# A four-layer graph network on one core: prologue, hand-overs and last store put in another order

## The chip, the core and the metric

The kernel runs on one core of a Trainium2 chip. The core has TensorE (matrix products, with a separate weight load that overlaps them), VectorE, ScalarE, GpSimd, and SyncE, whose queue here issues every DMA. Results of TensorE land in eight banks of 128 x 512 fp32. The metric is the device time of one execution in microseconds, as the median of several.

## The reference, cut to what matters

x is 128 graphs of 64 nodes with 512 features, fp32; adj is 128 matrices of 64 x 64. Four layers follow, each `x = x + layer(relu(layernorm(x)), adj)`:

```python
# layer 0:  w = ISQ * sum_d q * (adj @ k)          q, k = h @ Wqk;  x += softmax_nodes(w) * (h @ Wv)
# layer 1:  p = adj * exp(query @ key.T)           query, key, value with biases;  x += (p / rowsum(p)) @ value
# layer 2:  8 heads of 64: softmax(q @ k.T / 8 * (adj + adj)) @ v, with biases, then Wo and bo
# layer 3:  e = leaky_relu(sj + si + ab);  P = adj * exp(e) / rowsum;  H = h@Wk0 + P@h@Wk1 + P@P@h@Wk2 + sum(bk)
#           x += relu(H);   si, sj = (h @ Wv + bv) @ aw
```

The kernel folds weights: layer 0 needs only m0 = Wq Wk^T, layer 1 only a1 = Wk^T Wq with the vectors crow (from bq and Wk) and ucol (from bk and Wq) and the number s0 = bq . bk. In layer 3, sj and si come from two sums of h against two rows ("sums").

## The kernel before, in words

The 8192 rows are worked through in 16 groups of 512 (NG = 16), a group as 4 tiles of 128 rows, that is 8 graphs. Layers 0 and 1 go through one loop (group g of layer 0 beside group g - 1 of layer 1), then a loop of layer 2, then one of layer 3; x goes to memory in between (mid). Every engine has a program of its own, written out by hand in order, and waits on counting semaphores. Banks are taken strictly in turn, eight in rotation: whoever takes a bank waits until the use eight takes earlier was read out (`Banks.take`, line 51).

An fp32 product of full accuracy is made from three fp32r passes: each operand is split into a high part (ScalarE's copy, line 973) and a low part, the rest (VectorE, line 615, or GpSimd, lines 1204 and 1222); `gemm_T` (line 317) and `gemm` (line 327) run hi*hi, hi*lo, lo*hi. The prologue instead uses plain fp32 products, which are two records each in the trace (line 307).

The features go from x through statistics (VectorE, 627 and 629), a scale (GpSimd, 1209 to 1214), a normalising copy (ScalarE, 987), VectorE's transposes of 32 x 32 blocks (648), a gather by 16 DMAs (1406), then the high and low split, to the products.

The places that the change touches:

- Prologue of TensorE (lines 386 to 411): 32 transposes of Wqk in two halves (294), all copied out by ScalarE into qT and kTw; the small biases; product m0; s0; two row vectors (409) of bcol against wk1 and wq1; two of the four parts of a1. Round 0 then runs G0 (the first products of layer 0) and v0; at its end come the other two parts of a1, the transposes of Wv1, and the two row vectors are spread into crow (470) and ucol (474).
- Prologue of GpSimd: the low split of Wv0 (1240) before that of h0T (1241).
- Last round of layers 0 and 1 (g == NG): Wq2 is transposed and split, then `l01_pv` of group 14, then the last g1 (layer 1's product against a1), then Wk2 is transposed and split, then the last v1.
- Layer 2's scores (484): two calls, each for two tiles, each over all four feature blocks of q and k.
- Layer 2's last round: VectorE makes the sums of tiles 2 and 3 of group 0 (961), then adds the bias into the values VV (893), against which TensorE runs ctx (528).
- Layer 3: the sums go out to memory (`sums_out3`, 1431) and come back spread over all partitions (`sums_in3`, 1438); VectorE adds them (zct, 832), ScalarE takes exp, GpSimd multiplies with adj (alt), TensorE takes row sums (582), VectorE divides (900, 902), GpSimd scales (ttt, 1324), then Thi (ScalarE) and Tlo (VectorE), which the first hop (588) needs. The sums of group 1 are made in two pieces, one before layer 3's first low split Z_lo, one behind the row sums. On SyncE's queue the sums go out behind the next group's x load (`load3`) and four block loads.
- The last store is one DMA of 1 MB behind the last of four tiles.

Of the kernel before, what the change touches and what calls it, by code (L numbers as in the profile page):

```python
# [74 lines left out]
def build(nc, x, adj, nodemask, L0_gnn_Wqk, L0_gnn_Wv, L1_gnn_Wq_w, L1_gnn_Wq_b, L1_gnn_Wk_w, L1_gnn_Wk_b,  # L75
# [14 lines left out]
    with root:  # L90
# [20 lines left out]
        d_o = sems("x_out0 x_out1 x_out2 x_out3")  # L111
        d_adj = sems("adj_in0 adj_in1")
# [8 lines left out]
        (c_pool, a_whi, v_wlo, p_wlo, a_qkT) = sems("consts_pool w_hi w_lo_dve w_lo_pool qkT")  # L121
        (v_mcol, v_rows1, v_crow, v_ucol, p_one1) = sems("mcol rows1 crow ucol ones_v")
# [65 lines left out]
        urow, crow1 = alloc(tmp, "urow", [1, 512]), alloc(tmp, "crow1", [1, 512])  # L188
# [73 lines left out]
        def x_slot(k):  # L262
            return k % 4
# [22 lines left out]
        def pe_program(eng):  # L286
# [99 lines left out]
            pe.wait_ge(c_pool, 1)  # L386
            for half in range(2):
                pe.wait_ge((d_qk0, d_qk1)[half], 16)
                for cc in range(4):
                    transposed_blocks(("qkT", half, cc), wqk[:, :, half * 512:(half + 1) * 512], cc, (a_qkT, 4 * half + cc + 1))  # L390
# [6 lines left out]
            pe.wait_ge(a_qkT, 8)  # L397
            product("m0", qT, kTw)
            b, full, before = bank.take(("s0",), (v_rows1, 1))
# [27 lines left out]
            for g in range(NG + 1):  # L427
# [3 lines left out]
                else:  # L431
# [5 lines left out]
                    split_T("q2", Wq2["raw"])  # L437
                if on_pv:
                    l01_pv(g - 2)
# [10 lines left out]
                if on1:  # L450
# [12 lines left out]
                else:  # L463
                    product("a1", wk1, wq1, (2, 3))
                    pe.wait_ge(d_v1, 16)
                    split_T("v1", wv1)
                    b, full, before = bank.take(("crow",), (v_crow, 1))
                    pe.wait_ge(*before)
                    pe.wait_ge(v_rows1, 3)
                    eng.matmul(b[:], ones1[0:1, :], crow1[:], start=True, stop=True).then_inc(full, 1)  # L470
# [1132 lines left out]
```

## Time and profile before

| | |
|---|---|
| three runs | 2316.1, 2312.76, 2315.93 us; median 2315.93 |
| the profiled execution | 2312.03 us, of which 2310.2 are the span |
| TensorE busy | 2287.1 us, 99% of the span |
| VectorE, ScalarE, GpSimd busy | 57%, 32%, 30% |
| mean granted TensorE clock | 0.998 of full speed |
| DMA | 209.01 MB, mean 90 GB/s |
| chain that ended last | TensorE 93%, VectorE 2%, SyncE's queue 2%, rest 3% |

All times in the trace are microseconds from the span's start; 1.83 us of the execution lie around the span. A record's length overlaps with its neighbour's on TensorE, so there the distance between starts is what one costs.

### The profile page before, as it was taken

The numbers are of one execution on the slowest core, as the hardware profiler recorded it, in microseconds if no ns is written. First come the engines' busy times: TensorE is split into PE (matmuls) and PEld (weight loads), VectorE is DVE, ScalarE is ACT, GpSimd is POOL, SyncE is SP. The second block draws the span as 40 slices with busy tenths as digits, with TensorE's granted clock in tenths as the row PEclk, the third lists the DMA queues.
The fourth block names the chain that finished last, engine by engine and source line by source line (L and its number), as shares of the span: only waits on it lengthen the run. The fifth ranks groups of instructions, "written<-read, shape, count | busy, mean of one in ns | idle before, by whom it ended". The sixth has DMA issues, their size and how long they took to land.

```text
span 2310.2 us, 39569 instructions
## 1 busy us (share of the span) xinstructions
PE 2287.1 (99%) x16015; PEld 1860.6 (81%) x16015; DVE 1318.4 (57%) x2745; ACT 747.8 (32%) x1333; POOL 700.2 (30%) x930
## 2 busy tenths in 40 slices
PE   8999999999999999999999999999999999999998
PEld 5788788888878877888888888888778888888887
DVE  3565565656556555545554445555686757676753
ACT  3332323333233333333333333333433232323221
POOL 2433333343333322233322223332342121212120
PEclk9999999999999999999999999999999999999999
DMA  6323333333333343222232222222353333333330
GB/s 198 77 76 95 109 101 83 93 91 87 95 108 105 97 124 105 61 60 67 80 93 60 60 61 60 72 85 95 95 142 94 98 94 97 95 97 96 96 78 37
DMA packets 173479, 209.01 MB, mean 90 GB/s; under 512 B 64800, under 2 KB 81264, under 8 KB 173296
## 3 DMA queue, kind: packets, MB, share of 16 engines
q1 hardware_dynamic: 173296, 206.48, 32.0%
q8 instruction: 126, 2.06, 0.4%
q14 instruction: 57, 0.47, 0.1%
HBM read 88.91 MB, written 50.37 MB: 60 GB/s over the span
## 4 chain that ended last, share of the span: by engine, by line
PE 93%; DVE 2%; SPq 2%; ACT 1%; issue 1%; DMA 1%; POOL 0%; DVEq 0%; ACTq 0%
PE bank L327 50%; PE bank L317 29%; PE bank L588 4%; PE bank L343 3%; SPq L1406 2%; PE bank L528 1%; PE bank L501 1%; PE bank L307 1%; PE bank L378 1%; PE bank L511 1%; PE bank L294 0%; DVE hs L648 0%; DVE yt L961 0%; ACT g1T L1022 0%; PE bank L409 0%
## 5 line engine op out<-in xcount | busy, mean ns | idle before, releaser
L327 PE MATMUL bank<-w_hi,h3T_hi 128*128 128x512 f32 x768 | 302.4, 394 | 0.0
L327 PE MATMUL bank<-w_hi,h3T_lo 128*128 128x512 f32 x768 | 299.5, 390 | 0.0
L327 PE MATMUL bank<-w_lo,h3T_hi 128*128 128x512 f32 x768 | 299.5, 390 | 0.0
L615 DVE TENSOR_TENSOR Z_lo<-bank,Z_hi 128x512 fp32r<-128x512 f32 x128 | 87.1, 682 | 181.6 <-ACT Z_hi L973 181.3
L987 ACT ACTIVATE hn<-x,stA 128x512 f32<-128x512 f32 x192 | 140.7, 804 | 99.3 <-POOL stA L1214 99.3
L327 PEld LDWEIGHTS bank<-w_hi,h3T_hi 128*128 128x128 f32 x768 | 144.6, 188 | 30.2
L327 PEld LDWEIGHTS bank<-w_lo,h3T_hi 128*128 128x128 f32 x768 | 144.4, 188 | 30.2
L327 PEld LDWEIGHTS bank<-w_hi,h3T_lo 128*128 128x128 f32 x768 | 144.4, 188 | 30.2
L973 ACT ACTIVATE Z_hi<-bank 128x512 fp32r<-128x512 f32 x128 | 76.1, 596 | 251.1 <-PE bank L327 159.6
L1209 POOL TENSOR_SCALAR stA<-stA 128x4 f32<-128x4 f32 x48 | 11.5, 241 | 448.1 <-DVE stA L629 446.9
L615 DVE TENSOR_TENSOR cT_lo<-bank,cT_hi 128x256 fp32r<-128x256 f32 x128 | 44.7, 409 | 179.7 <-ACT cT_hi L973 179.7
L1222 POOL TENSOR_TENSOR h3T_lo<-hGA,h3T_hi 128x512 fp32r<-128x512 f32 x64 | 80.8, 1295 | 202.6 <-ACT h3T_hi L973 202.6
L1222 POOL TENSOR_TENSOR h1T_lo<-hGB,h1T_hi 128x512 fp32r<-128x512 f32 x64 | 80.7, 1293 | 201.2 <-ACT h1T_hi L973 201.2
L627 DVE BATCH_NORM_STATS2 stA<-x 128x6 f32<-128x512 f32 x192 | 128.2, 668 | 9.7 <-DMA x<-mid 9.1
L648 DVE STREAM_TRANSPOSE hs<-hn 128x512 f32<-128x512 f32 x192 | 120.6, 682 | 10.2 <-ACT hn L987 9.8
L805 DVE TENSOR_TENSOR x<-bank,x 128x512 f32<-128x512 f32 x64 | 43.3, 677 | 135.2 <-PE bank L327 132.1
L973 ACT ACTIVATE g0T<-bank 128x512 f32<-128x512 f32 x64 | 38.3, 598 | 239.9 <-PE bank L317 239.9
L327 PE MATMUL bank<-v_hi,h0T_hi 128*128 128x512 f32 x256 | 104.5, 408 | 0.0
L327 PE MATMUL bank<-o2w_hi,cT_hi 128*128 128x512 f32 x256 | 103.5, 404 | 0.5 <-DVE cT_lo L615 0.5
L1286 POOL TENSOR_TENSOR x<-x,blk 128x512 f32<-128x512 f32 x64 | 80.7, 1299 | 73.3 <-ACT hn L987 73.3
L317 PE MATMUL bank<-h1T_hi,a_hi 128*128 128x512 f32 x256 | 99.8, 390 | 2.4 <-POOL h1T_lo L1222 2.4
L317 PE MATMUL bank<-h0T_hi,m_hi 128*128 128x512 f32 x256 | 101.7, 397 | 0.0
(222 smaller groups left out, 5824.9 us busy)
## 6 DMA issues: line engine op xcount, KB each, us to landing
hGA<-hs SPq DMA_DIRECT2D x768, 64.0 KB, 2.0
mid<-x SPq DMA_DIRECT2D x32, 1024.0 KB, 4.8
x<-mid SPq DMA_DIRECT2D x32, 1024.0 KB, 5.8
x<-in_x SPq DMA_DIRECT2D x16, 1024.0 KB, 5.7
hGB<-hs SPq DMA_DIRECT2D x256, 64.0 KB, 2.0
out<-x SPq DMA_DIRECT2D x16, 1024.0 KB, 5.4
blk<-in_adj SPq DMA_DIRECT2D x128, 64.0 KB
adj<-in_adj SPq DMA_DIRECT2D x64, 64.0 KB, 3.3
```

Source lines behind the costliest of these rows:

```text
L317: ins = eng.matmul(b[:], W[l][:, k, os], h[r][:, k, :], start=(k == 0 and i == 0), stop=(k == 3 and i == 2))
L327: ins = eng.matmul(b[:], h[l][:, k, ts], W[r][:, k, :], start=(k == 0 and i == 0), stop=(last and k == 3 and i == 2))
L343: ins = eng.matmul(b[h, t * 64:(t + 1) * 64], left[:, k, ts], right[:, 2 * i:2 * i + 2, 4 * k + t, :], start=(k == 0), stop=(k == 3))
L588: ins = eng.matmul(b[:], T[g % 2][l][:, t, :], Z[zi][r][:, t, :], start=False, stop=(i == 2))
L615: return eng.tensor_tensor(lo, src, hi.bitcast(F), ALU.subtract)
L627: m = dve.step(eng.bn_stats(st[:, t, 0:6], xt[:, t, :]))
L648: eng.transpose(hs[:, :, :, t, :].rearrange("p b c r -> p c b r"), (hn1 if layer == 1 else hn)[t][:].rearrange("p (c b r) -> p c b r", c=4 ...
L973: return eng.activation(dst, src, ACT.Copy)
L987: eng.activation(h[t][:], xt[:, t, :], ACT.Relu, bias=st[:, t, 10:11], scale=st[:, t, 9:10]).then_inc(done, 1)
L1222: eng.tensor_tensor(by_token(h["lo"], q), hG[:, q], by_token(h["hi"], q).bitcast(F), ALU.subtract).then_inc(done, 1)
L1286: eng.tensor_tensor(xt[:, t, :], xt[:, t, :], bo2, ALU.add).then_inc(p_xb, 1)
L1406: eng.dma_start(hG[b * 32:b * 32 + 32, q].rearrange("p c r -> p (c r)"), hs[q * 32:q * 32 + 32, b].rearrange("p c t r -> p (c t r)")).then ...
```

## The change

What it does, part by part:

1. TensorE transposes the unit matrix 20 times into a bank that nobody reads, before it waits for Wqk. The k half of Wqk is copied out by VectorE, the q half by ScalarE as before.
2. crow comes at once in all partitions, from 4 products with a broadcast column as weights; ucol comes as columns, from 16 products with one column each. The two row vectors and what was done with them at the end of round 0 fall away.
3. One part of a1 instead of two is made before G0, three instead of two behind it. GpSimd splits h0T before Wv0.
4. Wk2 is transposed and split right behind Wq2, ahead of `l01_pv` and g1, on TensorE, VectorE and ScalarE.
5. Scores: one call for all four tiles, which runs the first two feature blocks for all tiles, then the last two, and waits for q and k by halves.
6. In layer 2's last round the values are added before the sums; the sums of layer 3's group 1 are made in one piece.
7. Sums go out ahead of the loads on SyncE's queue. The last group's store is four DMAs of 256 KB, one behind each tile.

Lines in parentheses stand for several.

```diff
@@ pe_program
             pe.wait_ge(c_pool, 1)
+            b, full, _ = bank.take(("idle",), (c_pool, 1))
+            for i in range(20):
+                ins = eng.transpose(b[:, 0:128], ident[:], ident[:])
+            ins.then_inc(full, 1)
             for half in range(2):
                 pe.wait_ge((d_qk0, d_qk1)[half], 16)
                 for cc in range(4):
-                    transposed_blocks(("qkT", half, cc), ..., cc, (a_qkT, 4 * half + cc + 1))
+                    transposed_blocks(("qkT", half, cc), ..., cc, ((a_qkT, v_qkT)[half], cc + 1))
...
-            pe.wait_ge(a_qkT, 8)
+            pe.wait_ge(a_qkT, 4)
+            pe.wait_ge(v_qkT, 4)
             product("m0", qT, kTw)
...
-            for j, (w, loaded, c0) in enumerate(((wk1, d_k1, 0), (wq1, d_q1, 4))):
-                b, full, before = bank.take(("rows1", j), (v_rows1, 2 + j))
-                pe.wait_ge(*before)
-                pe.wait_ge(loaded, 16)
+            b, full, before = bank.take(("crow",), (v_crow, 1))
+            pe.wait_ge(*before)
+            pe.wait_ge(d_k1, 16)
+            for k in range(4):
+                ins = eng.matmul(b[:], bcol[:, k:k + 1].to_broadcast([128, 128]), wk1[:, k, :], start=(k == 0), stop=(k == 3))
+            ins.then_inc(full, 1)
+            b, full, before = bank.take(("ucol",), (v_ucol, 1))
+            pe.wait_ge(*before)
+            pe.wait_ge(d_q1, 16)
+            for d in range(4):
                 for k in range(4):
-                    ins = eng.matmul(b[0:1, :], bcol[:, c0 + k:c0 + k + 1], w[:, k, :], start=(k == 0), stop=(k == 3))
-                ins.then_inc(full, 1)
-            product("a1", wk1, wq1, (0, 1))
+                    ins = eng.matmul(b[:, d:d + 1], wq1[:, k, d * 128:(d + 1) * 128], bcol[:, 4 + k:5 + k], start=(k == 0), stop=(k == 3))
+            ins.then_inc(full, 1)
+            product("a1", wk1, wq1, (0,))
...
                     split_T("q2", Wq2["raw"])
+                    pe.wait_ge(d_k2, 16)
+                    split_T("k2", Wk2["raw"])
                 if on_pv:
                     l01_pv(g - 2)
...
-                    if g == NG:
-                        pe.wait_ge(d_k2, 16)
-                        split_T("k2", Wk2["raw"])
                     l01_v1(g - 1, 0)
...
-                    product("a1", wk1, wq1, (2, 3))
+                    product("a1", wk1, wq1, (1, 2, 3))
                     pe.wait_ge(d_v1, 16)
                     split_T("v1", wv1)
-                    (crow: ones1[0:1, :] x crow1; ucol: four urow x ones1[0:1, 0:1])
...
-            def l2_scores(g, u):
+            def l2_scores(g):
                 bs = []
-                for r in range(2):
+                for r in range(4):
...
-                pe.wait_ge(a_q, 4 * g + 4)
-                pe.wait_ge(a_k, 4 * g + 4)
-                for x_ in range(2):
-                    t = 2 * u + x_
-                    for mm in range(2):
+                for mm in range(2):
+                    pe.wait_ge(a_q, 4 * g + 2 * mm + 2)
+                    pe.wait_ge(a_k, 4 * g + 2 * mm + 2)
+                    for t in range(4):
                         for a in range(2):
...
                             for s in range(2):
                                 for p in range(2):
-                                    h, m, (b, full) = HALF[p], 2 * mm + s, bs[p]
+                                    h, m, (b, full) = HALF[p], 2 * mm + s, bs[2 * (t // 2) + p]
...
-                                    if x_ == 1 and mm == 1 and a == 1 and s == 1:
+                                    if mm == 1 and t % 2 == 1 and a == 1 and s == 1:
                                         ins.then_inc(full, 1)
@@ dve_program
+            for cc in range(4):
+                dve.wait_ge(*bank.done(("qkT", 1, cc)))
+                eng.tensor_copy(kTw[:, cc, :], bank.of(("qkT", 1, cc))[:]).then_inc(v_qkT, 1)
             dve.wait_ge(*bank.done(("cols",)))
...
-            for j, row in enumerate((crow1, urow)):
-                dve.wait_ge(*bank.done(("rows1", j)))
-                eng.tensor_copy(row[:], bank.of(("rows1", j))[0:1, :]).then_inc(v_rows1, 1)
-            split_W(Wa1, "a1", (0, 1))
+            (crow and ucol copied here instead of at the end of round 0)
+            split_W(Wa1, "a1", (0,))
...
                     split_W(Wq2, "q2")
+                    split_W(Wk2, "k2")
                 if on_pv:
                     l01_x2(g - 2)
...
                 if on1:
                     adj_T(0, g - 1)
-                    if g == NG:
-                        split_W(Wk2, "k2")
...
                 if not on:
-                    l3_sums(dve, eng, 1, (0, 1))
+                    l3_sums(dve, eng, 1, range(4))
                 if on:
                     dve.wait_ge(d_bv2, 16)
-                    if g == NG - 1:
-                        l3_sums(dve, eng, 0, (2, 3))
                     for t in range(4):
                         (the additions of bv2 into VV)
+                    if g == NG - 1:
+                        l3_sums(dve, eng, 0, (2, 3))
...
                     if g == 0 and t == 0:
                         l3_rowsum(0)
-                        l3_sums(dve, eng, 1, (2, 3))
@@ act_program
-            for half, dst in enumerate((qT, kTw)):
-                for cc in range(4):
+            for cc in range(4):      (qT alone)
...
                     features2_hi(1, NG - 1, hT[1], (3,))
+                    split_W(Wk2, "k2")
...
                         g1(g - 1)
-                    if g == NG:
-                        split_W(Wk2, "k2")
@@ pool_program
+            features_lo(0, 0, hT[0], hGA, p_flo0)
             split_in_place(Wv0, "v0")
-            features_lo(0, 0, hT[0], hGA, p_flo0)
@@ sp_program
                         sp.wait_ge(*bank.done(("wT", "a1", 3)))
-                        sp.wait_ge(*bank.done(("rows1", 1)))
+                        sp.wait_ge(*bank.done(("ucol",)))
...
             for g in range(NG):
+                sums_out3(g + 1)
                 load3(g + 2)
                 load_blocks(3, g + 1)
-                sums_out3(g + 1)
                 sums_in3(g + 1)
                 gather(3, g + 2)
-                sp.wait_ge(v_x4, 4 * g + 4)
-                store_x(kA(3, g), out_v[g])
+                if g + 1 < NG:
+                    sp.wait_ge(v_x4, 4 * g + 4)
+                    store_x(kA(3, g), out_v[g])
+            for t in range(4):
+                sp.wait_ge(v_x4, 4 * (NG - 1) + t + 1)
+                eng.dma_start(out_v[NG - 1][:, t, :], xs[x_slot(kA(3, NG - 1))][:, t, :]).then_inc(d_last, 16)

```

## Rows read from the trace of the kernel before

**Rows 1.** TensorE's waits: releaser, then total us, times, longest us.

```profile
PE bank L317 <- POOL h1T_lo L1222: 2.4, 2, 1.6
PE bank L528 <- DVE VV L893: 2.3, 1, 2.3
PE bank L588 <- DVE Tlo L615: 2.3, 1, 2.3
...
PE bank L317 <- DVE h2T_lo L615: 0.7, 1, 0.7
```

**Rows 2.** Timeline of TensorE, 0 to 140 us: start, length, line, operation.

```profile
5.83 5.67 PE L294 MATMUL bank<-ident,wqk 128*128 128x128 f32 x32 [5.83 <-DMA wqk<-in_L_gnn_Wqk]
...
12.34 14.00 PE L307 MATMUL bank<-kTw,qTw 128*128 128x512 f32 x32 [0.49 <-ACT kTw L973]
...
26.38 3.59 PE L409 MATMUL bank<-wk,bcol 128*1 128x512 f32 x8
...
33.34 7.13 PE L307 MATMUL bank<-wq,wk 128*128 128x512 f32 x16
39.91 0.79 PE L317 MATMUL bank<-h0T_hi,m_hi 128*128 128x512 f32 x1
...
73.62 1.12 PE L470 MATMUL bank<-crow,ones 1*128 1x512 f32 x2
74.58 0.94 PE L474 MATMUL bank<-ones,urow 1*128 1x1 f32 x8
75.45 0.50 PE L317 MATMUL bank<-h0T_hi,m_hi 128*128 128x512 f32 x1
```

**Rows 3.** Timeline of ScalarE, 5.7 to 12.4 us, one row of four.

```profile
8.66 0.60 ACT L973 ACTIVATE qTw<-bank 128x512 f32<-128x512 f32 x1 [0.25 <-PE bank L294]
```

**Rows 4.** Windows: busy time by engine, granted clock, DMA share, GB/s.

```profile
6.70:7.60 0.90, 0.90 (x6) 0.90 (x6) 0.00 (x0) 0.60 (x1) 0.00 (x0) 1.00 1.04 385
```

**Rows 5.** Source view of the two loads of Wqk, time from issue.

```profile
L1443 SPq DMA_DIRECT2D wqk<-in_L_gnn_Wqk x2: 445/470/496, 0.7 to 1.2; - x2
...
DMA to landing us min/median/max: 5.0/6.1/7.2
```

**Rows 6.** Timeline of all engines, 0 to 75 us, GpSimd.

```profile
32.48 4.95 POOL L1222 TENSOR_TENSOR h0T_lo<-hGA,h0T_hi 128x512 fp32r<-128x512 f32 x4
```

**Rows 7.** Timelines of ScalarE and VectorE, 828 to 925 us.

```profile
839.74 0.63 ACT L973 ACTIVATE h1T_hi<-hGB 128x512 fp32r<-128x512 f32 x1 [0.20 <-DMA hGB<-hs]
...
854.77 2.48 DVE L615 TENSOR_TENSOR k2w_lo<-bank,k2w_hi 128x512 fp32r<-128x512 f32 x4 [4.58 <-PE bank L294]
```

**Rows 8.** Timelines, 1600 to 1740 us, and a window of line 961 alone.

```profile
1682.42 0.87 DVE L832 TENSOR_TENSOR zct<-sirows,stB 64x256 f32<-64x256 f32 x2 [1.15 <-DMA sirows<-si]
...
1684.80:1687.40 2.60, 2.54 (x8) 1.00 0.46 107
...
1692.09 0.85 ACT L973 ACTIVATE Thi<-ttt 64x256 fp32r<-64x256 f32 x2 [3.22 <-POOL ttt L1324]
...
1697.71 1.41 DVE L615 TENSOR_TENSOR Tlo<-ttt,Thi 64x256 fp32r<-64x256 f32 x2
```

**Rows 9.** SyncE's queue: two issues near 1670 us, its waits after 1800 us.

```profile
1663.30 0.37 SPq L1431 DMA_DIRECT2D si<-stB  x1
...
1676.19 0.62 SPq L1438 DMA_DIRECT2D sirows<-si  x1
...
SPq L1438 <- DMA si<-stB: 122.9, 12, 12.8
```

**Rows 10.** Timelines of TensorE and VectorE, 886 to 915 and 990 to 1064 us.

```profile
894.58 2.09 PE L501 MATMUL bank<-KK,QQ 64*64 64x64 f32 x128 [0.87 <-ACT KK L1101]
...
1006.53 3.00 DVE L615 TENSOR_TENSOR h2T_lo<-hGA,h2T_hi 128x512 fp32r<-128x512 f32 x4
...
1012.34 0.48 PE L317 MATMUL bank<-h2T_hi,q2w_hi 128*128 128x512 f32 x1
```

**Rows 11.** Source view of the last three stores.

```profile
DMA to landing us min/median/max: 4.3/4.3/5.0
```

More of the change, by code:

```diff
@@ L111, in build @@
         d_o = sems("x_out0 x_out1 x_out2 x_out3")
+        (d_last,) = sems("last_out")
         d_adj = sems("adj_in0 adj_in1")
@@ L396, in pe_program @@
             eng.transpose(b[:, 64:72], brow1[:], ident[0:8, 0:8]).then_inc(full, 1)
-            pe.wait_ge(a_qkT, 8)
+            pe.wait_ge(a_qkT, 4)
+            pe.wait_ge(v_qkT, 4)
             product("m0", qT, kTw)
-            b, full, before = bank.take(("s0",), (v_rows1, 1))
+            b, full, before = bank.take(("s0",), (v_s0, 1))
             pe.wait_ge(*before)
@@ L463, in pe_program @@
                 else:
-                    product("a1", wk1, wq1, (2, 3))
+                    product("a1", wk1, wq1, (1, 2, 3))
                     pe.wait_ge(d_v1, 16)
                     split_T("v1", wv1)
[L467 to L470, printed above, removed]
-                    b, full, before = bank.take(("ucol",), (v_ucol, 1))
-                    pe.wait_ge(*before)
-                    for d in range(4):
-                        ins = eng.matmul(b[:, d:d + 1], urow[:, d * 128:(d + 1) * 128], ones1[0:1, 0:1], start=True, stop=True)
-                    ins.then_inc(full, 1)
             def l2_gemm_T(n, g, W, freed):
@@ L563, in pe_program @@
                 if on:
-                    for u in range(2):
-                        l2_scores(g, u)
+                    l2_scores(g)
                 if prev:
@@ L722, in dve_program @@
             dve.wait_ge(*bank.done(("s0",)))
-            eng.tensor_reduce(s0, bank.of(("s0",))[:, 0:4], AX, ALU.add).then_inc(v_rows1, 1)
-            for j, row in enumerate((crow1, urow)):
-                dve.wait_ge(*bank.done(("rows1", j)))
-                eng.tensor_copy(row[:], bank.of(("rows1", j))[0:1, :]).then_inc(v_rows1, 1)
-            split_W(Wa1, "a1", (0, 1))
+            eng.tensor_reduce(s0, bank.of(("s0",))[:, 0:4], AX, ALU.add).then_inc(v_s0, 1)
+            dve.wait_ge(*bank.done(("crow",)))
+            eng.tensor_copy(crow[:], bank.of(("crow",))[:]).then_inc(v_crow, 1)
+            dve.wait_ge(*bank.done(("ucol",)))
+            eng.tensor_copy(ucol, bank.of(("ucol",))[:, 0:4]).then_inc(v_ucol, 1)
+            split_W(Wa1, "a1", (0,))
             for g in range(NG + 1):
@@ L785, in dve_program @@
                 else:
-                    dve.wait_ge(*bank.done(("crow",)))
-                    eng.tensor_copy(crow[:], bank.of(("crow",))[:]).then_inc(v_crow, 1)
-                    dve.wait_ge(*bank.done(("ucol",)))
-                    eng.tensor_copy(ucol, bank.of(("ucol",))[:, 0:4]).then_inc(v_ucol, 1)
                     l01_dots(0)
@@ L1030, in norm_B @@
                     norm(hn1, stB, p_stB, 4 * g + t + 1, a_nB, xs[x_slot(kA(0, g))], t)
-            for half, dst in enumerate((qT, kTw)):
-                for cc in range(4):
-                    act.wait_ge(*bank.done(("qkT", half, cc)))
-                    copy(dst[:, cc, :], bank.of(("qkT", half, cc))[:]).then_inc(a_qkT, 1)
+            for cc in range(4):
+                act.wait_ge(*bank.done(("qkT", 0, cc)))
+                copy(qT[:, cc, :], bank.of(("qkT", 0, cc))[:]).then_inc(a_qkT, 1)
             norm_A(0, 0)
```

24 lines of the change are left out of this document (12 added, 12 removed).

## The prediction

> **What bounds the kernel now.** I read the page's busy shares first (in the table above: TensorE 99%), then the list of what TensorE waited for, then TensorE's own order of instructions in the prologue, and last the other engines' timelines around each wait. The reader is to see two things. TensorE is the bound nearly everywhere, so an edit pays only where it takes away a TensorE instruction, takes away one of its few waits, or shortens what lies before its first or behind its last instruction. And the waits are few and single: four rows of the list carry most of what can be won inside the kernel [rows 1], the longest single ones being 1.6, 2.3, 2.3 and 0.7 us. The prologue is 39.9 us of TensorE work before the first big product [rows 2].
>
> **The prologue, step by step.** *Unit transposes and the split copies.* The 32 transposes of Wqk start at 5.83, when its first half has landed, and product m0 starts at 12.34 [rows 2]. ScalarE copied one bank of four transposes in 0.60 us and then waited 0.25 us for TensorE [rows 3], so the first transposes came at 0.85/4 = 0.21 us each. All 32 took 5.67 us, so the second 16 took about 2.3 us, 0.14 each. The same instruction became quicker while TensorE was kept busy, so I take it that 20 unit transposes, run while the load is under way, let all 32 go at the quick pace. The granted clock of that early stretch is shown as 1.00, the 2.4 GHz level [rows 4]; by that row alone nothing was held back, unit transposes would change nothing, and only the second engine for the copies would be left, some 0.2 us. The Trainium skill (TensorE: Matmul & The Clock Gate, "What's actually happening") says that the array's clock starts at the lower level, 1.2 GHz, and is released by sustained activity; by that rule the step is worth the whole 0.6 that follows. The quick pace puts the q half at 8.1. The k half was issued about 0.5 us after the first (0.72) and the longest landing is 7.2 us [rows 5]: it is there at about 8.4, so its 16 transposes end at 10.6. Its copies are now VectorE's; a 128x512 tile out of a bank goes there at 2.48/4 = 0.62 us [rows 7], so four from 9.1 end at 11.6, and m0 starts at 11.7: **0.6 us gained** (bounds 0 and 1.5, the whole difference in pace).
>
> *Biases by columns.* Now two rows of 4 products (16 records) take 33.34 - 26.38 = 6.96 us, 0.435 each [rows 2]. After: the broadcast crow is 8 such records, 3.5 us; ucol is 16 products of one column, 32 records. The nearest row is the old ucol, also 128 weight columns against one column: 8 records from 74.58 to 75.45, 0.109 each [rows 2], so 32 cost 3.5 us. Sum 7.0: **nothing gained**. Bounds: the weights had one row there and have 128 now, so twice the price is possible (3.5 lost); free, it would be 3.5 gained. What was done with the results at the end of the first round, 73.62 to 75.45 [rows 2], goes: **1.83 us gained**.
>
> *One part of a1 ahead of G0.* Two parts take 39.91 - 33.34 = 6.57 us [rows 2]. One of them moves from before G0 to behind it: nothing gained or lost, if G0 can start 0.6 + 3.3 us earlier, at 36.0. GpSimd's low part of h0T ends at 32.48 + 4.95 = 37.4 now [rows 6], 1.4 us too late, but it stood behind four equally long pieces of Wv0 and is put ahead of them; it can then be held by ScalarE and the gather alone, about 1.2 us (one of its four pieces) behind the last slice. Wv0's pieces end 5 us after that, under G0's 48 matmuls (at half of a1's 0.41 us a record still 9.8 us). The cover of the first is thin: without it 1.4 us are lost.
>
> **Wk behind Wq.** The last g1 waits 1.6 us for h1T_lo [rows 1]; 16 transposes at 0.109, 1.75 us, are moved into that hole. But their banks come free only through ScalarE's high and VectorE's low parts, and g1's first bank now is that of k2's third. ScalarE ends its last h1T slice at 840.37 [rows 7]; then 0.6 for k2's first high part and three low parts of 0.62 make 842.9 with the semaphores. Now g1 can start behind one low piece of 1.24 us on GpSimd [rows 6], at 841.7. So 1.75 - 1.2 = **0.5 us gained** (0 to 1.75). VectorE's x2 behind it comes 3 us later; its stores have a round to go.
>
> **Scores.** Only round 0 waits for KK, 0.87 us of the 2.09 us row [rows 10]. The first half of the scores can now run in that wait. VectorE gets its first two banks after 3/4 instead of 1/2 of the scores, about 895.1 instead of 895.6, and the next thing late is h2T_lo at the end of VectorE's softmax (0.7 us wait [rows 1]), which moves by that 0.5: **0.45 us gained** (0 to 0.87). In the other 15 rounds the same order costs VectorE 0.5 us; h2T_lo ends at 1006.53 + 3.00 = 1009.5 and TensorE asks for it at 1012.34 [rows 10], 2.8 us later, so nothing.
>
> **Values ahead of sums, sums together, sums sent first.** The 2.3 us wait for VV goes, as VectorE adds the four values (4 x 0.62) first. But TensorE then reaches the wait for Tlo (2.3 us [rows 1]) sooner, and what ends that wait is not TensorE's. Its chain: the sums go out at 1663.30, come back by a load issued at 1676.19 [rows 9], zct runs at 1682.42 as soon as they land; later Thi is ready at 1692.94, but Tlo starts only at 1697.71 and ends at 1699.12 [rows 8], since four sums stand between. So 4.8 us of the chain are sums. Moved ahead of the row sums, four cost 2.5 us where GpSimd is quiet [rows 8]; part of that falls into time in which VectorE waits there for TensorE, and I take 2.0 (bounds 0 and 2.5) by which Thi comes later; Tlo follows at once: 4.8 - 2.0 = **2.8 us gained**, not 2.3 + 2.3. Values first sends the sums 2.5 us later, about 1666; the return load stood 12.9 us behind them on SP, while a later round's return waited 122.9/12 = 10.2 us on average, 12.8 at most [rows 9], so it can still leave near 1676. Bounds: 0.4 (12.8 us out, so return 2.4 later) and 5.6 (return 2.8 earlier, with TensorE no longer held). In later rounds SP now stands for the sums before its next x load and four block loads, about 1.5 us; TensorE needs neither for most of a round.
>
> **Store by tiles.** The last store, 1 MB, lands 4.3 us after its issue [rows 11]; the last quarter, 256 KB, lies between a quarter of that, 1.1, and the whole. Some of a transfer surely does not shrink with its size, so I take 2.5, a little under the middle: **1.8 us gained** (0 to 3.2). Only the last of the four is in the way; the others leave while TensorE still works. The Trainium skill speaks against the split (DMA: Bandwidth & Descriptors, "Bandwidth"): batch transfers to 1 MiB or more, small ones waste most of their time. By that rule the four would cost more together, and the term were 0 if that reached the last; by the page's fit of 2.0 us and bytes over 436 GB/s, an estimate, the last falls from 4.4 to 2.6 us, again 1.8.
>
> **Sum:** 0.6 + 0 + 1.83 + 0.5 + 0.45 + 2.8 + 1.8 = 8.0 us. On the profiled execution's own 2312.0 that gives 2304.0. The median of the three runs, 2315.9, lies 3.9 above that execution; on it the sum gives 2307.9. The forecast lies between, **2306**.
>
> **Rivals.** *The hand-over is released wholly:* the sums return 3 us earlier, TensorE alone sets the first hop, 5.6 instead of 2.8: gain 11, about 2303. For it: SP reaches the return load sooner once the x stores move up. Against it: two 1 MB transfers share that stretch. *The sums' way through memory eats the hand-over:* out 2.5 us later and 12.8 us under way, return 2.4 later, 0.4 instead of 2.8: gain 5.6, 3.8 if the tail gives nothing: 2308.5 to 2310. *ucol's weight loads cost double:* gain 4.5, 2309.5; for it, a full 128 rows were never loaded against one column in a long row here. *Slower:* the new score order breaks the overlap of the small products. 128 records take 2.09 us, 16 ns each, against 0.109 us for lone small products; at 32 ns each a round costs 2.1 us more, 34 us in 16 rounds: 2340. It decides from 0.8 us a round on (8.0 + 4.6 over 16). Against it: the four innermost products that run beside each other stay as they were.
>
> **Chances and range.** Forecast case 0.58; released wholly 0.10; sums eat it 0.20; ucol double 0.07; slower 0.05. A measurement can tell 0.2%, 4.6 us, from no change. Faster: 0.58 + 0.10 + 0.12 of the third case = 0.80; same: 0.08 + 0.07 = 0.15; slower 0.05. Low end: the second case on the profiled execution, 2301; high end: the small gains on the median, 2311.5.
>
> **What would show it.** Right: ScalarE's and VectorE's Wqk copies side by side, m0 at 11.7, G0 near 36, round 1's G0 near 73.3; VV no longer in TensorE's waits, Tlo still there with about 2.5 us; KK gone; g1's last wait at bank or high parts of k2; the last store some 2.5 us. Wrong: TensorE waiting for h0T_lo before G0, 32 ucol records above 5 us, a score block longer than 2.1 us, zct later than now by itself.

## The result and the profile after

| | kernel before | changed kernel |
|---|---|---|
| median of 5 runs each, side by side | 2313.2 us | 2394.8 us |
| ratio, 95% interval | | 1.0353 [1.0338, 1.0368] |
| profiled execution | 2312.0 us | 2394.5 us |
| its span, mean granted clock | 2310.2 us, 0.998 | 2392.7 us, 0.987 |

The forecast was 2306; the kernel became 82 us slower. The two spans differ by 82.5 us, and TensorE's timeline splits that at four marks. Round 1's G0 starts 2.6 us sooner than before (72.88 against 75.45, [rows 2]). From there to the last transposition of layer 2 it loses 0.3. From that to the first hop of layer 3 it loses 2.8 (39.7 us where before spends 37.0). The rounds of layer 3 and the last store take 693.0 instead of 611.0 us: 82.0 lost. So the question is layer 3's rounds.

TensorE's list of waits, changed kernel (total us, times, longest); it answers to [rows 1]:

```profile
PE bank L581 <- POOL alt L1314: 59.6, 15, 5.5
...
PE bank L327 <- DVE cT_lo L614: 2.1, 1, 2.1
...
PE bank L501 <- issue: 1.5, 1, 1.5
```

VV, KK and the long wait for h1T_lo are gone, as forecast; Tlo, said to stay with about 2.5 us, has 0.2. The new first row was in no case of mine: the row sum, two records a round, waits for alt in 15 rounds.

One round of layer 3 in the changed kernel, rows of four engines' timelines (SPq is SyncE's queue), in order of time:

```profile
2001.49 0.41 SPq L1347 DMA_DIRECT2D out<-x  x1
2002.97 0.37 SPq L1426 DMA_DIRECT2D si<-stB  x1
2003.39 1.30 SPq L1344 DMA_DIRECT2D x<-mid  x1
2004.73 2.81 SPq L1362 DMA_DIRECT2D blk<-in_adj  x4
...
2013.74 0.35 SPq L1433 DMA_DIRECT2D sirows<-si  x1
...
2018.58 0.69 DVE L626 BATCH_NORM_STATS2 stA<-x 128x6 f32<-128x512 f32 x1 [7.42 <-DMA x<-mid]
...
2031.42 0.83 DVE L830 TENSOR_TENSOR zct<-sirows,stB 64x256 f32<-64x256 f32 x2
...
2033.23 0.72 POOL L1314 TENSOR_TENSOR alt<-ec,atc 128x256 f32<-128x256 f32 x1 [9.31 <-ACT ec L1116]
...
2034.01 0.70 PE L581 MATMUL bank<-alt,bones 128*128 128x256 f32 x2 [3.80 <-POOL alt L1314]
```

Read it from below. TensorE stands 3.80 us for alt. alt comes from ec, ec from zct, and zct is late although its rows had been asked for at 2013.74: it stands in VectorE's program behind the statistics of x, the transpositions of that x and the low parts of Z. The statistics began only at 2018.58, after 7.42 us in which VectorE waited for the x load. That load had been issued at 2003.39, right behind the sums. The two waits go together: in 12 of the 14 rounds with an x load the wait for alt is the idle time ahead of the statistics less 3.6 us (7.42 and 3.80 here, 6.36 and 2.74, 8.24 and 4.62). So the chain bears 3.6 us of lateness and passes on the rest.

How long the two transfers took, medians over 1900 to 2250 us (count, KB each, us from issue to landing):

```profile
x<-mid SPq DMA_DIRECT2D x8, 1024.0 KB, 15.6
...
si<-stB SPq DMA_DIRECT2D x8, 2.0 KB, 11.3
```

The wait is not the whole price. A window right behind a row sum that had waited (TensorE's busy us and records, granted clock, DMA share, GB/s):

```profile
1990.10:1994.90 4.80, 4.80 (x15) 0.64 0.47 109
```

and as much of the kernel before, at the same place in a round:

```profile
1950.24:1955.04 4.80, 4.80 (x23) 1.00 0.43 100
```

15 records in 4.8 us at a mean granted clock of 0.64, where the kernel before has 23 at 1.00. From 1768.20 to 2301.70 there are 12 rounds of 44.5 us, against 38.56: 5.9 us more, of which 4.2 are the wait (the 13 waits from 1768.20 on hold 55 us) and some 1.7 the slow records behind it. That is 71 us; the round that ends at 1768.20, which also waits 3.8 us for Z_lo, has 11.5 more and the round behind the twelve 2.9, while the end of the kernel gives 2.3 back.

The prologue, TensorE's timeline from 0 to 140 us, and the start of round 1's G0, for [rows 2]:

```profile
1.51 4.53 PE L389 MATMUL bank<-ident 128*128 128x128 f32 x20 [1.51 <-POOL ident L1229]
5.84 2.56 PE L294 MATMUL bank<-ident,wqk 128*128 128x128 f32 x16
...
11.90 13.97 PE L307 MATMUL bank<-kTw,qTw 128*128 128x512 f32 x32 [1.00 <-DVE kTw L715]
...
29.36 3.63 PE L420 MATMUL bank<-bcol,wq 128*128 128x1 f32 x32
32.85 3.68 PE L307 MATMUL bank<-wq,wk 128*128 128x512 f32 x8
35.97 0.79 PE L317 MATMUL bank<-h0T_hi,m_hi 128*128 128x512 f32 x1
...
72.88 0.48 PE L317 MATMUL bank<-h0T_hi,m_hi 128*128 128x512 f32 x1
```

Here the forecast holds within 0.4 us: m0 at 11.90 (11.7 said), ucol 3.49 us to the start of a1 (3.5), G0 at 35.97 (36.0), round 1's G0 at 72.88 (73.3).

The hand-over, timelines of SyncE, VectorE and TensorE, for [rows 8, 9]:

```profile
1665.77 0.37 SPq L1426 DMA_DIRECT2D si<-stB  x1
...
1668.16 0.43 SPq L1347 DMA_DIRECT2D mid<-x  x1
1668.69 0.45 SPq L1537 DMA_DIRECT2D w_raw<-in_L_gnn_Wk  x1
1675.10 0.34 SPq L1433 DMA_DIRECT2D sirows<-si  x1
...
1685.41 0.87 DVE L830 TENSOR_TENSOR zct<-sirows,stB 64x256 f32<-64x256 f32 x2 [7.61 <-DMA sirows<-si]
...
1688.05 1.22 PE L581 MATMUL bank<-alt,bones 128*128 128x256 f32 x2 [4.00 <-POOL alt L1314]
```

The sums leave 2.5 us later than before, though all that stands ahead of them has become some 4 us earlier: VectorE's softmax ends at 1655.6 instead of 1659.7. The values take 3.3 us of the difference. The rest is that the four sums now run beside GpSimd's low part of h3T, from 1659.27 to 1665.72. One of them there, and one of the kernel before:

```profile
1659.44 1.76 DVE L958 SCALAR_TENSOR_TENSOR yt<-hn,arowt 128x512 f32<-128x512 f32 x1
```

```profile
1661.67 0.68 DVE L961 SCALAR_TENSOR_TENSOR yt<-hn,arowt 128x512 f32<-128x512 f32 x1
```

The four take 5.8 us instead of 3.3. Their return is asked for 1.1 us sooner, at 1675.10, and yet zct comes 3.0 later, and now TensorE waits 4.00 us there. "zct later than now by itself" was the sign that I had named for this step being wrong. The return took 10.3 us, behind two transfers of 1 MB that now follow the sums within 3 us. The landings in that stretch, 1655 to 1692 us:

```profile
w_raw<-in_L_gnn_Wk SPq DMA_DIRECT2D x1, 1024.0 KB, 15.6
...
sirows<-si SPq DMA_DIRECT2D x1, 256.0 KB, 10.3
```

In the kernel before the same two take 9.3 and 6.2: there the sums had left 8.6 us ahead of the first 1 MB transfer.

The end: the last result is written by VectorE from 2389.47 to 2390.16 and the span ends at 2392.7, 2.6 us later; before it is 4.8.

### The profile page after: what moved, and what is told of

Same layout as the page of the kernel before. It is cut to its first block and busy times, and to the rows that moved or that the text cites. A ratio compares the mean times of both kernels' runs of the same rounds, so it can differ in the third digit from the quotient of the medians.

```text
span 2392.7 us, 39654 instructions
## 1 busy us (share of the span) xinstructions
PE 2314.7 (97%) x16049; PEld 1880.4 (79%) x16049; DVE 1316.9 (55%) x2747; ACT 742.5 (31%) x1329; POOL 698.0 (29%) x930
## 5 line engine op out<-in xcount | busy, mean ns | idle before, releaser
L327 PE MATMUL bank<-w_hi,h3T_hi 128*128 128x512 f32 x768 | 312.7, 407 | 0.0
L327 PE MATMUL bank<-w_lo,h3T_hi 128*128 128x512 f32 x768 | 307.2, 400 | 0.0
L327 PE MATMUL bank<-w_hi,h3T_lo 128*128 128x512 f32 x768 | 305.8, 398 | 0.0
L327 PEld LDWEIGHTS bank<-w_lo,h3T_hi 128*128 128x128 f32 x768 | 149.6, 195 | 32.2
L327 PEld LDWEIGHTS bank<-w_hi,h3T_hi 128*128 128x128 f32 x768 | 149.7, 195 | 32.0
L327 PEld LDWEIGHTS bank<-w_hi,h3T_lo 128*128 128x128 f32 x768 | 149.4, 195 | 32.3
L1204 POOL TENSOR_SCALAR stA<-stA 128x4 f32<-128x4 f32 x48 | 11.5, 239 | 529.3 <-DVE stA L628 529.2
L317 PE MATMUL bank<-h2T_hi,q2w_hi 128*128 128x512 f32 x256 | 101.0, 395 | 1.2 <-DVE h2T_lo L614 1.1
L1281 POOL TENSOR_TENSOR x<-x,blk 128x512 f32<-128x512 f32 x64 | 80.7, 1296 | 73.4 <-ACT hn L984 73.3
```

The source lines that it names most:

```text
L317: ins = eng.matmul(b[:], W[l][:, k, os], h[r][:, k, :], start=(k == 0 and i == 0), stop=(k == 3 and i == 2))
L327: ins = eng.matmul(b[:], h[l][:, k, ts], W[r][:, k, :], start=(k == 0 and i == 0), stop=(last and k == 3 and i == 2))
L1204: pool.step(eng.tensor_scalar(off, mean, -1.0, None, ALU.mult))
L1281: eng.tensor_tensor(xt[:, t, :], xt[:, t, :], bo2, ALU.add).then_inc(p_xb, 1)
```

## Experiments

In all kernels the parts not named are those of the changed kernel. Times are medians; ratios are to the kernel before, run beside each on the same chip.

| | edit | us | before, us | ratio, 95% interval |
|---|---|---|---|---|
| 1 | sums behind the loads | 2312.7 | 2312.4 | 0.9998 [0.9989, 1.0007] |
| 2 | kernel before, sums ahead | 2403.4 | 2312.4 | 1.0387 [1.0373, 1.0401] |
| 3 | only the wait ahead | 2315.2 | 2312.4 | 1.0008 [0.9999, 1.0017] |
| 4 | sums between x and blocks | 2331.7 | 2312.4 | 1.0078 [1.0054, 1.0103] |
| 5 | 1 + round 0's sums first | 2305.9 | 2312.8 | 0.9969 [0.9958, 0.9981] |
| 6 | 5 + round 1's sums split | 2312.4 | 2312.8 | 0.9998 [0.9989, 1.0007] |
| 7 | 1 + ucol interleaved | 2309.2 | 2312.8 | 0.9985 [0.9977, 0.9994] |
| 8 | sums ahead, 128 pieces | 2306.8 | 2312.8 | 0.9974 [0.9963, 0.9985] |
| 9 | 8 + strided read | 2310.1 | 2316.3 | 0.9975 [0.9966, 0.9984] |
| 10 | 9 + ucol interleaved | 2309.3 | 2316.3 | 0.9971 [0.9960, 0.9981] |
| 11 | 10 + round 0's sums first | 2304.2 | 2316.3 | 0.9950 [0.9938, 0.9963] |
| 12 | 9, sums behind | 2307.2 | 2316.3 | 0.9962 [0.9950, 0.9975] |
| 13 | sums on ScalarE's queue | 2353.8 | 2317.4 | 1.0161 [1.0146, 1.0177] |
| 14 | sums ahead, 256 pieces | 2323.5 | 2317.4 | 1.0032 [1.0019, 1.0044] |

**1. The sums behind the loads again.**

```
             for g in range(NG):
-                sums_out3(g + 1)
                 load3(g + 2)
                 load_blocks(3, g + 1)
+                sums_out3(g + 1)
```

> The changed kernel with one line put back: in layer 3's rounds the sums' transfer is issued behind the x load and the four block loads again; every other part of the change stays. Theory A (the x load stands behind the sums' 512 four-byte pieces in SP's queue, lands some 15 us after its issue instead of under 10, and all of the loss comes from it): a round of layer 3 takes 38.6 us again instead of 44.2, the row sums no longer wait for alt, and the time is 2306 to 2313, under or at the kernel before. Rival B (the loss comes from another part, the order of values and sums or the scores): it stays above 2380.

The same stretch as above, timelines of this kernel, and the landing of x over 1900 to 2250 us:

```profile
2004.33 0.51 SPq L1344 DMA_DIRECT2D x<-mid  x1
...
2008.24 0.71 SPq L1426 DMA_DIRECT2D si<-stB  x1
...
2013.25 0.68 DVE L626 BATCH_NORM_STATS2 stA<-x 128x6 f32<-128x512 f32 x1
...
2032.21 0.59 PE L581 MATMUL bank<-alt,bones 128*128 128x256 f32 x2
...
x<-mid SPq DMA_DIRECT2D x8, 1024.0 KB, 8.7
```

x lands in 8.7 us, statistics and row sum wait for nothing, and a round takes 38.56 us (1993.65 to 2032.21). One line made the whole loss: theory A, against B. (The profiled execution took 2318.7 us, 6 over the median; one late round in it waits 1.9 us for alt.) But the kernel is no faster than before; where the forecast 8 us went is asked by 5 to 7.

**2. That line alone, in the kernel before.** The edit of 1 the other way round, in the old code.

> The kernel before with that one line alone moved: the sums' transfer ahead of the x load and the block loads in layer 3's rounds. Theory A: the whole loss, 2313 + 78 to 85 = 2391 to 2398, a round of 44.2 us. Rival C (the late x hurts only together with another part of the change): under 2340.

91 us slower: the line needs no other part to do its harm. The expectation was 5 us short of that.

**3. The wait without the transfer.**

```
-                sums_out3(g + 1)
+                if g + 1 < NG:
+                    sp.wait_ge(v_sc, g + 2)
                 load3(g + 2)
                 load_blocks(3, g + 1)
+                sums_out3(g + 1)
```

> The changed kernel with SP's wait for the sums left ahead of the x load, but the transfer itself issued behind the x and block loads. Theory A (what delays x is the order of the transfers in the queue): like the undo of that line, 2306 to 2315, as the wait is about 1.1 us and x then lands some 11 us after the store. Rival D (the load is late since SP stands for the sums): near the changed kernel, above 2380.

SP's standing for the sums, the cost that I had written down in the prediction (1.5 us a round, hidden), is 1.1 us here (2001.53 to 2002.63 in one round) and shows as nothing: the interval overlaps that of 1, and the rounds take 38.56 us. What hurts is the transfer.

**4. Sums between x and blocks.**

> The changed kernel with the sums' transfer between the x load and the four block loads. Theory A (order: only what stands behind the sums comes late): x is in time and the blocks are late by some 5 us; the time is within 4 us of the undo of that line if nothing needs the blocks earlier. Rival E (the small pieces slow whatever is in flight, ahead or behind): x still lands 13 us or more after its issue, and the time stays above 2350.

A miss for both theories: 19 us slower than 1, far from 2350. In the profiled execution, which took 2339.8 us, x lands in 9.8 us by the median, but in 6 of 14 rounds VectorE waits 4 to 9.4 us for it, as here, 16 us behind its issue:

```profile
2016.04 0.51 SPq L1344 DMA_DIRECT2D x<-mid  x1
2017.08 0.63 SPq L1426 DMA_DIRECT2D si<-stB  x1
...
2032.14 0.69 DVE L626 BATCH_NORM_STATS2 stA<-x 128x6 f32<-128x512 f32 x1 [7.11 <-DMA x<-mid]
```

So a load that stands 1 us ahead of the pieces isn't safe from them. What tells the late rounds from the others stays open.

**13. The sums on another queue.** ScalarE issues them, SP only waits for them and loads x.

```
                     l3_zhi(0, ("z2", g, t), g, t)
+                    if t == (g == 0) and g + 1 < NG:
+                        act.wait_ge(v_sc, g + 2)
+                        eng.dma_start(si_dr[g + 1]..., scol[(g + 1) % 2][:, :, 1], ...)
...
-                sums_out3(g + 1)
+                if g + 1 < NG:
+                    sp.wait_ge(v_sc, g + 2)
```

> The changed kernel, with the sums of layer 3's rounds 1 to 15 issued by ScalarE on its own queue as soon as they are ready, while SP waits for the same sums and then issues the x load and the blocks; 512 pieces of four bytes, as in the changed kernel. Theory Q (x stands behind the pieces in its own queue): x lands 8 to 10 us after its issue, 2308 to 2318. Theory S (the pieces keep the DMA engines busy that all queues share): x lands 12 us or more after its issue, above 2350.

The queues of this kernel over 1900 to 2250 us (packets, MB, share of the 16 engines' time) and its landings:

```profile
q10 hardware_dynamic: 4752, 0.02, 0.9%
...
x<-mid SPq DMA_DIRECT2D x9, 1024.0 KB, 13.0
...
si<-stB ACTq DMA_DIRECT2D x9, 2.0 KB, 13.4
```

x still lands 4.3 us later than in 1, with nothing ahead of it in its own queue but the store; against 6.9 later in the changed kernel. So most of the delay comes from engines that the queues share (theory S, by x and by the time, 2353.8, which lies above its 2350), and the rest may be the order in the queue or the slightly later start of the pieces: not told apart. The Trainium skill (DMA: Bandwidth & Descriptors, "Issuing engines are not separate DMA queues") says that transfers issued by different engines run on the same 16 DMA engines and interleave; the 13.0 us agrees.

**8 and 14. Fewer pieces, still ahead of the load.** On each partition the four tiles' sums are laid out beside each other and sent as 128 pieces of 16 bytes, or 256 of 8. The rows come back in a wrong order, at the same work. The edit of 8:

```
-        scol = [late[...].rearrange("p (t c) -> p t c", c=2) for i in range(2)]
+        scol = [late[...].rearrange("p (c t) -> p t c", c=2) for i in range(2)]
-                    eng.dma_start(si_dr[g].rearrange("(t p) -> p t", p=128), ...)
+                    eng.dma_start(si_dr[g].rearrange("(p t) -> p t", t=4), ...)
```

> The changed kernel, sums' transfer still ahead of the loads, but sent as 128 pieces of 16 bytes instead of 512 of 4; the sums reach the rows in a wrong order, so the weights of layer 3 are wrong, at the same work. Theory A1 (the number of pieces sets how long the x load stands): x lands 4 us sooner, 11 us after its issue, and the time is 2310 to 2330. Rival A2 (any transfer of that kind ahead of the load costs the same): above 2380.

> The changed kernel with the sums ahead as 256 pieces of 8 bytes; the rows come back in a wrong order, so the weights of layer 3 are wrong, at the same work. With 512 pieces x landed 15.6 us after its issue, with 128 pieces 8.4. If the delay goes with the number of pieces, about 10.8, and as the row sums bore up to 3.7 us of idle ahead of the statistics with at most 0.2 of waiting: 2305 to 2318. If any form with over 128 pieces costs the same, above 2380.

Landings over 1900 to 2250 us, 128 pieces:

```profile
x<-mid SPq DMA_DIRECT2D x8, 1024.0 KB, 8.4
...
si<-stB SPq DMA_DIRECT2D x9, 2.0 KB, 4.4
```

and 256 pieces:

```profile
x<-mid SPq DMA_DIRECT2D x8, 1024.0 KB, 10.6
...
si<-stB SPq DMA_DIRECT2D x9, 2.0 KB, 6.0
```

The same 2 KB in 512, 256 and 128 pieces lands x in 15.6, 10.6 and 8.4 us, and behind the load in 8.7. The price goes with the pieces, not with the 2 KB or the place: theory A1, though with 128 pieces less is left of it than expected (8.4 and 2306.8, for 11 and 2310 to 2330). The number of pieces and their size change together here, and are not told apart. The transfer's own time shows the same where nothing else is in flight ahead of it, at the hand-over; landings from 1655 to 1692 us with 512 pieces (changed kernel), 256 (14) and 128 (12):

```profile
si<-stB SPq DMA_DIRECT2D x1, 2.0 KB, 9.3
```

```profile
si<-stB SPq DMA_DIRECT2D x1, 2.0 KB, 4.0
```

```profile
si<-stB SPq DMA_DIRECT2D x1, 2.0 KB, 1.4
```

With 256, x's 10.6 was met but the time came out 5 us above the expected range, on a chip where the kernel before takes 5 us longer too: the row sum waited in 9 rounds, 1 us or so each, with 4.3 us of idle ahead of the statistics on average, and again the one is the other less 3.6 us. The Trainium skill (DMA: Bandwidth & Descriptors, "Rules for kernel authors") warns that a strided last dimension becomes one descriptor an element; here the count of packets under 512 B over those 350 us, in which nine sums leave, falls from 8048 (kernel of 1) to 4592 with 128 pieces, 3456 = 9 x 384: one packet a piece, which agrees.

**9 and 12. Made right.** The rows come back in another order, and VectorE reads them with a stride; 12 has the sums behind the loads.

```
-                    eng.tensor_tensor(zc[h, :, :], si[h, :, h], ...
+                    eng.tensor_tensor(zc[h, :, :], si[:].rearrange("p t n -> p (t n)")
+                                      .rearrange("p (n t) -> p t n", t=4)[h, :, h], ...
```

> The changed kernel, whole, with the sums' transfer ahead of the loads as 128 pieces of 16 bytes, and VectorE reading the rows that come back with a stride of four elements, so that the weights of layer 3 are right again. The kernel with the pieces alone ran 2306.8. Theory A1 (the number of pieces): 2305 to 2309. Rival K (the strided read of the rows costs VectorE more than 0.5 us a round, on the way to alt): 2310 or more, and zct longer than the 0.83 us it takes in the changed kernel.

> The kernel with 128 pieces and the strided read, with the sums' transfer behind the x load and the blocks. It tells what sending the sums ahead is worth once their transfer is short: theory A1, nothing in the rounds, as nothing there waits for the rows: within 1.5 of the one with the sums ahead. If the early sums do help the rounds, 3 or more slower.

9 has the ratio of 8; its 2310.1 lies at rival K's bound, but on a chip where the kernel before takes 3.5 us longer. The strided read does make zct longer, 1.19 us a round instead of 0.83, less than the 0.5 us that K asked for, and no row sum behind the first rounds waits for it. 12 is 2.9 us under 9 by the medians, more than the 1.5 expected, with intervals that overlap. Sending the sums ahead is worth nothing in the rounds, even when it is cheap.

**5 and 6. The order at the hand-over.** In 5, VectorE takes `l3_sums(dve, eng, 0, (2, 3))` ahead of the four values again; in 6 round 1's sums are split again too.

```
                     dve.wait_ge(d_bv2, 16)
+                    if g == NG - 1:
+                        l3_sums(dve, eng, 0, (2, 3))
                     for t in range(4):
...
-                    if g == NG - 1:
-                        l3_sums(dve, eng, 0, (2, 3))
```

> The kernel of the first experiment (sums' transfer behind the loads) with round 0's sums of layer 3 put back ahead of the last values on VectorE; round 1's stay together. It ran 2312.7, and between the last transposition of layer 2 and the first hop of layer 3 it spends about 41 us where the kernel before spends 37. Theory H (with the values first, the sums leave 2.5 us later, their way through memory then sets alt, and the row sum waits 4 to 5 us for it): the wait for alt goes, a 2.3 us wait for the values comes back, the stretch falls to 37 or 38, and the time to 2309 to 2311. Rival F (another engine sets that stretch): no change, 2312 to 2313.

> The same with round 1's sums of layer 3 split again as in the kernel before, so that the whole order of values and sums is the old one. Theory H: the stretch is that of the kernel before, 37 us, with the waits for the values and for Tlo of 2.3 each; 2309 to 2311. If the joined sums of round 1 are what hurts, this is 2 us or more faster than the one with only round 0 put back; if they help, up to 2 slower.

5 gains 0.3%, some 7 us over 1, more than theory H had expected: the stretch from the last transposition to the first hop falls to 35.9 us from 40.9 in 1 (37.9 to 42.3 in the six profiles with that order and 512 pieces), and the wait for VV that should have come back with 2.3 us has 0.8. VectorE's softmax now ends 2.1 us ahead of the first transposition of that block instead of 0.6, which the new score order, kept in 5, may have brought. The sums leave at 1660.47, 10 us ahead of the 1 MB store, and the weights behind it land in 8.2 us, where they take 16.8 in 1. 6 loses that gain: joining round 1's sums pays, as forecast, by 6.5 us where up to 2 had been expected, more than the wait. TensorE's timeline of 6 shows why:

```profile
1698.26 0.53 PE L587 MATMUL bank<-Z_hi,Thi 128*128 128x512 f32 x1 [2.29 <-DVE Tlo L614]
...
1699.87 0.63 PE L327 MATMUL bank<-w_lo,h3T_hi 128*128 128x512 f32 x1
1700.29 0.63 PE L327 MATMUL bank<-w_hi,h3T_lo 128*128 128x512 f32 x1
```

Behind the 2.29 us wait for Tlo, records follow each other at 0.43 us instead of 0.23. In 5 and 6 the stretch is 35.9 and 37.4 us; the rest of 6's loss lies in two waits for alt in later rounds, 3.7 us in all, and what follows them.

**7 and 10. ucol interleaved.** Each two a1 records of 512 columns are followed by eight of ucol's one-column records, in place of 32 in a row ahead of a1.

```
...
             for d in range(4):
+                m = eng.matmul(b2[:], wk1[:, d, 0:128], wq1[:, d, :], start=(d == 0), stop=(d == 3))
...
                 for k in range(4):
                     ins = eng.matmul(b[:, d:d + 1], wq1[:, k, ...], bcol[:, 4 + k:5 + k], ...)
...
-            product("a1", wk1, wq1, (0,))
```

> The kernel of the first experiment with the 32 one-column records of ucol interleaved with a1's 8 records of 512 columns, 8 behind each pair, instead of standing in a row ahead of them. Theory G (the row of one-column records lets the granted clock fall to 0.5 in some executions, so that a1 and the first product behind it take up to 3.5 us longer): the clock stays at 1.00 in that stretch, round 1's first product starts at 73 us instead of 75 to 76.4, and the median falls by 1 to 3, to 2309.5 to 2311.5, with less spread. Rival J (the clock falls for another reason): the clock still falls there, 2312 to 2313.

> The same with the one-column records of ucol interleaved with a1's. Theory G (the clock falls behind a row of one-column records): granted clock 1.00 from 27 to 41 us, round 1's first product at 73 us instead of 75, 1.5 to 3.5 faster than without: 2302.5 to 2306. If the fall has another cause: no change.

The window 33 to 37 us, behind ucol, first in the kernel of 1 (records in a row):

```profile
33.00:37.00 4.00, 4.00 (x7) 0.50 0.97 297
```

and in 7 (interleaved):

```profile
33.00:37.00 4.00, 4.00 (x25) 1.00 0.90 293
```

In 1, TensorE sits at the lower level, 1.2 GHz, for that window, and a1's eight records take 6.56 us instead of the 3.68 shown above. Of eleven profiled kernels with ucol's records in a row ten show 0.50 to 0.68 there; the changed kernel's own profile is the one at 1.00. All three interleaved ones show 1.00. What TensorE did before it fell was the row of one-column products; a mix with 512-column ones holds the clock: theory G. Round 1's G0 then starts at 73.3, 73.0 and 72.9 us, instead of 74.6 to 76.5. In the time, 7 shows 3.5 us against 1, with intervals that just overlap; 10 against 9 shows 0.8, well within the intervals and short of the 1.5 to 3.5 expected. So the clock's fall is shown, and that the whole time gains by its going is not clear of noise.

**11. Both, with 128 pieces.** 10 with the edit of 5.

> The same again with round 0's sums of layer 3 put back ahead of the last values. Theory H says that this order paid only since the sums' way through memory set alt; with the quick transfer the values should come first: slower than without by 0 to 2.5, 2303 to 2308. If the order pays in itself, 2 or more faster, 2300 to 2303.

The fastest of all, 0.5% under the kernel before, and a miss for theory H: round 0's sums first pay 5 us with a quick transfer as well, by the medians. Its hand-over, SyncE, VectorE and TensorE:

```profile
1659.75 0.34 SPq L1430 DMA_DIRECT2D si<-stB  x1
...
1676.64 1.62 DVE L834 TENSOR_TENSOR zct<-sirows,stB 64x256 f32<-64x256 f32 x2 [0.29 <-DMA sirows<-si]
...
1683.19 0.59 PE L585 MATMUL bank<-alt,bones 128*128 128x256 f32 x2
```

The sums leave at once, no wait for alt is left there, and the wait for cT_lo falls from 2.7 us in 10 to 0.5: with the values first, the four sums stand between them and cT_lo on VectorE. The way through memory was only one of two costs of that order. The other is the time of the sums themselves, which run beside GpSimd there: the four take 6.3 us in 10, three of them 1.75 each, and 3.3 in 11.

## Why the prediction was wrong

**The failed step** is the last sentence on the sums: "In later rounds SP now stands for the sums before its next x load and four block loads, about 1.5 us; TensorE needs neither for most of a round." The first half is true and costs nothing (3). But the step moves a transfer past five others, the x load and four block loads, and I priced the queue's wait, not the transfer. [rows 9] held a hint: a return that waited 10.2 us on average for 2 KB, though there the pieces stood behind those loads. Alone, at the hand-over, the 512 pieces took 9.3. x then lands 6.9 us later than in 1, and TensorE's need of it is nearer than "most of a round": its statistics stand in VectorE's fixed order ahead of the low parts of Z and of zct, so a late x stops alt as well, and the slack between the two is 3.6 us. Twelve rounds at 5.9 us are 71 of the 82, and most of the rest lies in the rounds on either side of them. All of it was outside my range, and my "slower" rival named another mechanism, which did not come: 15 of the 16 score blocks take 2.10 us, as before.

**The other terms, by what they measured.**

*Unit transposes and copies:* 0.4 of 0.6 in this pair of profiles, but that is not clear of the loads: m0 starts between 11.90 and 12.39 in the 14 profiles with this part, and at 12.34 and 12.10 in the two without it (before, 2). The pace did come as said: the unit transposes take the slow one on themselves, 0.22 us each, and those of Wqk go at 0.12 to 0.16. The k half then waits for its load, in most profiles, by up to 0.9 us. The pace, not the granted clock, shows this: that reads 1.00 there too. It agrees with the rule of the Trainium skill that the prediction cited (TensorE: Matmul & The Clock Gate, "What's actually happening"), and not with "nothing was held back".

*Biases by columns:* the size was right, 3.49 us, no double price; the cost that I had not thought of is behind it, the fall of the clock, 1.8 to 3.6 us in ten of eleven profiles (by round 1's G0). *End of round 0:* 1.83 forecast, and round 1's G0 comes at 72.9. The prediction wrote 73.3; its own terms, 0.6 and 1.83 ahead of 75.45, give 73.0.

*Wk and scores:* together 1.5 us gained at 1008 us (4.1 against 2.6 at 73), of 0.95 said. But in the last round the block of scores stops after 101 of its 128 records for 1.5 us for nothing that the trace shows ("issue"). It does so in every kernel here with the new order (1.0 to 2.7 us) and in neither with the old; its cause is open.

*Hand-over:* the sign was wrong, -2.8 for +2.8. The prediction had round 0's sums later by the four values alone, 2.5 us; the sums themselves also took 5.8 us instead of 3.3, beside GpSimd's low part of h3T. The rival "the sums' way through memory eats it" named the place but not the way: the return left sooner, not 2.4 us later, and then took 10.3 us instead of 6.2, behind a weight load that landed only in 15.6. I take it that the pieces of the sums held that load: it takes 8.9 us in 12, with 128 pieces in the same order. It is then the failed step's error a second time: the sums' pieces run into large transfers that they had been clear of. My lower bound, 0.4 gained, took no account of a new wait of 4.0 us and of the slow records behind it.

*Store by tiles:* 4.8 to 2.6 us, 2.3 gained of 1.8 said. That the small last transfer gains nothing, the reading against it, is refuted here. The fit that the prediction set beside it is given in the Trainium skill (DMA: Bandwidth & Descriptors, "Anatomy of one DMA — SWDGE (gpsimd) path") for transfers that GpSimd issues; SyncE issues these, and the last quarter lands in 2.0 us, not the 2.6 of that estimate.

With the one line put back, five of these terms stand, and still the kernel only equals the one before (1): the hand-over takes 40.9 us in that profile instead of 37.0 (39.9 in 3 and 37.9 in 7, with the same order), and the clock behind ucol takes the prologue's gain. Both causes were then removed one by one (5, 7), and both together with short pieces give the 0.5% of 11.

## What to carry to other kernels

Before a transfer is moved past another, count its pieces and look at its own time from issue to landing: two KB in 512 pieces hold a 1 MB load back by 6.9 us here, by 4.3 from another queue, and where an in-order engine stands for that load, everything behind it in its program is late too. A wait of a busy TensorE can cost more than its length, since the records behind it run slower for a while (2.3 us of wait and 1.8 behind it, 4.2 and 1.7); a row of one-column products can do the same to what follows, unless wide ones stand between them. Small values that must go through memory are best sent with neighbours together, and the reader's stride can put them right for 0.36 us of VectorE a round, which did not show in the time.

## What the hardware showed that was not expected

The pieces' own recorded time hides their price: in 13 the queue that carries only them shows 0.9% of the engines' time over 350 us, 0.01 us a packet, while the load beside them lands 4.3 us later.

TensorE idles 2.7 to 5.5 us in a round and its granted clock falls to the lower level behind that: a mean of 0.64 over 4.8 us behind the 3.29 at 1989.81. Only the shortest of the 13 waits, 2.74 us at 2257.37, leaves it at 1.00. It also falls without any idle time, behind 32 one-column records (0.50 to 0.68 over 33 to 37 us).

One of VectorE's sums of a 128x512 tile takes 0.64 to 0.69 us by itself and 1.75 beside GpSimd's low part of h3T, which itself takes 6.45 us for four pieces instead of 4.98. Moving the sums moved them beside that work.
